# Zero borders written a layer earlier, a residual loaded in four pieces, and three fp32r products for each fp32 product in an attention layer's front

## The reference, cut to what matters

```python
# layer 0: attention with a bias net, then an MLP
x = x + out_proj(attention(...))
x = x + mlp_w2 @ gelu(mlp_w1 @ bn(x) + b1) + b2          # 512 -> 2048 -> 512
# layer 1: deformable 3x3 convolution under a gate
d   = normalise(pointwise(depthwise3x3(x[:, :256])))     # mean and variance over the pixels
off = conv3x3(d, off_w)                                  # 18 channels: an offset (y, x) per tap
dc  = sum over 9 taps of dc_w[tap] @ bilinear(d at (y, x) + tap + off)
das = d * sigmoid(layernorm_channels(dc))
x   = x * das + x * g                                    # g: a gate from x[:, 256:]
# layer 2: linear attention
x   = x + gamma * ((Kf V) Qf / norm)
# layer 3: group norm, q, k, v, softmax attention, projection
h   = group_norm(x); q, k, v = W_qkv @ h + b
x   = x + W_out @ softmax(q k / 8) v
```

## Time and profile before

| | |
|---|---|
| median of 3 runs | 4279.25 us (4275.34 to 4280.5) |
| the profiled execution's own time | 4278.21 us |
| its span (first to last instruction) | 4276.4 us |
| PE, DVE, ACT, POOL busy | 91, 69, 60, 49% of the span |
| MLP stage ends, layer 1 begins | about 2721 us into the span |
| layer 1 ends, layer 2 begins | about 3438 us |
| front of layer 3, V and QK products | 3585 to 3751 us |

### The profile page before, as it was taken

One profiled execution on the slowest core, in us unless ns is written; L12 is line 12 of the kernel. 1 busy time (PEld: TensorE's weight loads), 2 busy tenths in 40 slices (PEclk: granted clock), 3 DMA queues, 4 the chain that ended last, 5 costly groups with the idle time before them and its releaser, 6 DMA issues. The chain is left out here.

```text
span 4276.4 us, 66562 instructions
## 1 busy us (share of the span) xinstructions
PE 3904.4 (91%) x18504; PEld 2388.6 (56%) x18504; DVE 2967.6 (69%) x4476; ACT 2575.5 (60%) x4592; POOL 2083.5 (49%) x1857
## 2 busy tenths in 40 slices
PE   5999999999999999999998999888779377969999
PEld 3555555555555555555556888547667243435553
DVE  7888888888888888888886333538898833235552
ACT  5899999999999999999994333322112420113331
POOL 0555555555555555555552555216676500036663
PEclk8999999999999999999999999989889677989999
DMA  1200000000000000000002000239999812453312
GB/s 48 101 12 10 9 9 11 10 10 9 9 12 9 10 9 9 12 10 9 9 9 82 1 1 1 79 101 377 367 370 393 299 47 71 145 128 70 70 41 79
DMA packets 146916, 326.80 MB, mean 76 GB/s; under 512 B 45736, under 2 KB 46760, under 8 KB 145788
## 3 DMA queue, kind: packets, MB, share of 16 engines
q1 hardware_dynamic: 105340, 174.46, 13.2%
q0 software_dynamic: 41472, 151.01, 9.0%
HBM read 246.14 MB, written 79.04 MB: 76 GB/s over the span
## 5 line engine op out<-in xcount | busy, mean ns | idle before, releaser
L557 POOL TENSOR_TENSOR cpb_sum<-cpb_tab 128x512 f32<-128x512 f32 x1028 | 1045.9, 1048 | 965.3 <-DVE cpb_r L687 965.0
L668 ACT ACTIVATE cpb_h<-cpb_z,net_vec 128x512 f32<-128x512 f32 x1536 | 1006.0, 697 | 50.5 <-PE cpb_z L608 37.9
L605 PE MATMUL cpb_z<-cpb_r,cpb_w2a 128*128 128x512 f32 x2048 | 858.5, 419 | 23.5 <-DVE cpb_h L728 23.5
L687 DVE SCALAR_TENSOR_TENSOR cpb_r<-cpb_sum,cpb_r 128x512 fp32r<-128x512 f32 x1024 | 695.5, 710 | 187.8 <-ACT cpb_r L662 187.8
L606 PE MATMUL cpb_z<-cpb_r,cpb_w2b 128*128 128x512 f32 x2048 | 801.1, 391 | 0.0
L608 PE MATMUL cpb_z<-cpb_r,cpb_w2a 128*128 128x512 f32 x2048 | 799.7, 390 | 0.0
L687 DVE SCALAR_TENSOR_TENSOR cpb_r<-cpb_z,cpb_r 128x512 fp32r<-128x512 f32 x1028 | 661.8, 685 | 160.4 <-ACT cpb_r L662 154.6
L662 ACT ACTIVATE cpb_r<-cpb_z 128x512 fp32r<-128x512 f32 x1028 | 560.5, 604 | 127.7 <-PE cpb_z L592 127.7
L662 ACT ACTIVATE cpb_r<-cpb_sum 128x512 fp32r<-128x512 f32 x1024 | 598.5, 648 | 2.0 <-POOL cpb_sum L557 2.0
L605 PEld LDWEIGHTS cpb_z<-cpb_r,cpb_w2a 128*128 128x128 f32 x2048 | 383.9, 187 | 365.8 <-issue 301.0
L1559 DVE SCALAR_TENSOR_TENSOR dc_acc<-dc_g,dc_wt,dc_acc 128x512 f32<-128x512 f32 x560 | 444.7, 800 | 58.0 <-DMA dc_g<-conv_out,dc_idx 42.0
(11 more groups left out here) (344 smaller groups left out, 5196.7 us busy)
## 6 DMA issues: line engine op xcount, KB each, us to landing
conv_out<-dc_ys SPq DMA_DIRECT2D x576, 64.0 KB, 6.1
cpb_log<-log_dram SPq DMA_DIRECT2D x66, 256.0 KB, 3.1
qk_parts<-gn_r SPq DMA_DIRECT2D x64, 256.0 KB, 2.0
dc_wr<-in_dc_wT SPq DMA_DIRECT2D x9, 1024.0 KB, 6.0
bias_dram<-cpb_bst SPq DMA_DIRECT2D x520, 8.0 KB
net_x<-in_x SPq DMA_DIRECT2D x8, 1024.0 KB, 9.4
sa_qa<-qk_parts SPq DMA_DIRECT2D x16, 512.0 KB
sa_ka<-qk_parts SPq DMA_DIRECT2D x16, 512.0 KB
```

The lines of the kernel that those rows point to most:

```text
L557: pool.tensor_tensor(SUM[:, r, :].rearrange("p (y x) -> p y x", x=W), TAB[:, slot, r, 0, :].unsqueeze(1).broadcast_to([P, NF // W, W]), TA ...
L605: pe.matmul(z2[:, bank, :], W2A[:], R1[:, k, :], start=True, stop=False)
L668: act.activation(H2[:, t % 8, :], z2[:, t % 3, :], ACT.Relu, bias=V("cpb_b2")).then_inc(h2a, 1)
L687: v.scalar_tensor_tensor(R2[:, t % RING, :], first_layer(t), 0.0, R1[:, t % RING, :].bitcast(F32), ALU.max, ALU.subtract).then_inc(r2_read ...
```

## The change

1. The border writes move from layer 1's SP list to the MLP stage's. There GpSimd clears a zero tile of half the width (128 x 256) first, SP writes 18 DMAs of the same bytes from it, and waits for them at the stage's end. In layer 1 weights(1) follows directly on the loads of OFW; GpSimd's and SP's waits for `borders` go.
2. In layer 1 GpSimd clears only the edge cells of DP that are read (two memsets of 544 and 512 values a partition) in place of the whole tile; ZERO's memset goes. ScalarE's wait for `zeroed` goes, TensorE waits for it before the offset convolution.
3. X comes back in four DMAs of 1 MB, a column block each: the first where the one of 4 MB was, the others when 129, 136 and 140 tiles have been sampled. VectorE waits for each piece before the first output of its block.
4. Layer 3's W_V and W_QK are split in high and low fp32r parts in layer 2: 12 casts of 128 x 512 on ScalarE after its work on image 0, 12 subtractions on GpSimd after column block 1. The low parts are written over the whole ones.
5. The front writes the normalised x as HH and HL (fp32r): ScalarE writes FULL (fp32, 128 x 512, a ring of four), VectorE casts it to HH and subtracts for HL, in 16 `parts`; six of them ahead of the V chunks, one after each of the first ten. V and QK are three fp32r products where there was one of fp32.

```diff
 def layer0_mlp
+        ZERO = s.sb("zero", [P, C // 2])
         @block.sync
+            sp.wait_ge(blank, 1)
+            for rows in itertools.chain(*g["conv_out"]):
+                for r0 in (0, HP * HP - edge):
+                    sp.dma_start(rows[r0:r0 + edge, :]..., ZERO[0:edge, :]...).then_inc(borders, 16)
+                sp.dma_start(middle..., ZERO[0:gaps, :]...).then_inc(borders, 16)
             for sem in g["spent"]:
                 sp.sem_clear(sem)
+            sp.wait_ge(borders, 16 * 18)
         @block.gpsimd
+            pool.memset(ZERO[:], 0.0).then_inc(blank, 1)
 def layer1
         @block.sync
-            for u in range(SLOTS):
-                for b in range(B):
-                    rows = table[u][b]
-                    sp.dma_start(rows[0:edge, :], ZERO[0:edge, :]).then_inc(borders, 16)
-                    sp.dma_start(rows[HP * HP - edge:, :], ZERO[0:edge, :]).then_inc(borders, 16)
-                    sp.dma_start(middle, ...).then_inc(borders, 16)
             weights(1)
...
             sp.wait_ge(y_mm, TILES)
-            sp.dma_start(X[:].rearrange("p t n -> p (t n)"), x_spill).then_inc(x_back, 16)
-            sp.wait_ge(borders, 16 * 3 * SLOTS * B)
+            for n, units in enumerate((0, LAST[1] + 1, LAST[2] - 4, LAST[3] - 4)):
+                cols = slice(n * NF, (n + 1) * NF)
+                if units:
+                    sp.wait_ge(sampled, units)
+                sp.dma_start(X[:, :, cols], x_spill.rearrange(...)[:, :, cols]).then_inc(x_back[n], 16)
         @block.gpsimd
-            pool.memset(DP[:], 0.0).then_inc(zeroed, 1)
+            pool.memset(images[:, :, 1:H + 3:H + 1, 1:W + 3], 0.0).then_inc(zeroed, 1)
+            pool.memset(images[:, :, 2:H + 2, 1:W + 3:W + 1], 0.0).then_inc(zeroed, 1)
             pool.memset(OFW[:], 0.0).then_inc(zeroed, 1)
-            pool.memset(ZERO[:], 0.0).then_inc(zeroed, 1)
...
-            pool.wait_ge(borders, 16 * 3 * SLOTS * B)
         @block.tensor
+            pe.wait_ge(zeroed, 3)
         @block.scalar
-            act.wait_ge(zeroed, 1)
         @block.vector
-                if n == 0 and m == 0:
-                    v.wait_ge(x_back, 16)
+                if m == 0:
+                    v.wait_ge(x_back[n], 16)
 def layer2
         @block.gpsimd
+                if n == 1:
+                    for i, (whole, high, low) in enumerate(PIECES):
+                        pool.wait_ge(split_h, i + 1)
+                        pool.tensor_tensor(low, whole, high.bitcast(F32), ALU.subtract).then_inc(split_l, 1)
         @block.scalar
+                if b == 0:
+                    act.wait_ge(weights_in, 64)
+                    for whole, high, low in PIECES:
+                        act.copy(high, whole).then_inc(split_h, 1)
 def layer3_front
         @block.tensor
+            def three(out, w, wl, x, xl, first, last):
+                pe.matmul(out, w, x, start=first, stop=False)
+                pe.matmul(out, wl, x, start=False, stop=False)
+                return pe.matmul(out, w, xl, start=False, stop=last)
             for i in range(CHUNKS):
-                pe.wait_ge(hn_a, CT // 2 * (i // NC + 1))
-                pe.wait_ge(hn_v, CT // 2 * (i // NC + 1))
...
                 for k in range(CT):
-                    mm = pe.matmul(pv[:, i % 2, :], HN[:, k, i * P:(i + 1) * P], WV[:, k, :], ...)
+                    if i % CT == 0:
+                        pe.wait_ge(hh_ready, i + k + 1)
+                        pe.wait_ge(hl_ready, i + k + 1)
+                    mm = three(pv[:, i % 2, :], HH[:, k, pix], HL[:, k, pix], WVH[:, k, :], WVL[:, k, :], ...)
...
-                        mm = pe.matmul(pq[:, m % RING, :], WQK[:, k, m * P:(m + 1) * P], HN[:, k, bass.ds(n * NF, NF)], ...)
+                        mm = three(pq[:, m % RING, :], WQH[:, k, of], WQL[:, k, of], HH[:, k, col], HL[:, k, col], ...)
         @block.scalar
+            for i in range(NT * CT):
+                n, m = divmod(i, CT)
+                if i >= CT:
+                    act.wait_ge(hl_ready, i - CT + 1)
+                act.activation(FULL[:, m, :], X[:, m, n * NF:(n + 1) * NF], ACT.Identity, ...).then_inc(full, 1)
         @block.vector
+            def parts(i):
+                n, m = divmod(i, CT)
+                v.wait_ge(full, i + 1)
+                v.tensor_copy(HH[:, m, col], FULL[:, m, :]).then_inc(hh_ready, 1)
+                v.wait_ge(hh_ready, i + 1)
+                v.tensor_tensor(HL[:, m, col], FULL[:, m, :], HH[:, m, col].bitcast(F32), ALU.subtract).then_inc(hl_ready, 1)
+            AHEAD = CT + 2
+            for i in range(AHEAD):
+                parts(i)
             v.sem_inc(r2_ready, RING)
             for i in range(CHUNKS):
...
                 v.tensor_tensor(VE[:, i % RING, :], pv[:, i % 2, :], BV[:], ALU.add).then_inc(v_ready, 1)
+                if i + AHEAD < NT * CT:
+                    parts(i + AHEAD)
```

More of the change, by code:

```diff
@@ L1 @@
 from contextlib import ExitStack
+import itertools
 import math
@@ L883, in layer0_mlp @@
         FULL = s.sb("full", [P, 2, NF])
+        ZERO = s.sb("zero", [P, C // 2])
+        blank, borders = s.sem("blank"), s.sem("borders")
         py = s.ps("py", [P, CT, NF])
@@ L911, in _ @@
         def _(sp):
+            sp.wait_ge(blank, 1)
+            HP = H + 4
+            edge, gaps = 2 * HP + 2, H - 1
+            for rows in itertools.chain(*g["conv_out"]):
+                for r0 in (0, HP * HP - edge):
+                    sp.dma_start(rows[r0:r0 + edge, :].rearrange("r (k c) -> r k c", k=2),
+                                 ZERO[0:edge, :].unsqueeze(1).broadcast_to([edge, 2, C // 2])).then_inc(borders, 16)
+                middle = rows[edge + W:edge + W + gaps * HP, :].rearrange("(y x) c -> y x c", x=HP)[:, 0:4, :]
+                sp.dma_start(middle.rearrange("y x (k c) -> y (x k) c", k=2),
+                             ZERO[0:gaps, :].unsqueeze(1).broadcast_to([gaps, 8, C // 2])).then_inc(borders, 16)
             for sem in g["spent"]:
                 sp.sem_clear(sem)
+            sp.wait_ge(borders, 16 * 18)
         @block.tensor
@@ L1125, in layer1 @@
         GA = s.sb("ga", [P, CT, B, 2])
-        ZERO, DCB = s.sb("zero", [P, C]), s.sb("dcb", [P, C])
+        DCB = s.sb("dcb", [P, C])
         LM, LR, LN = (s.sb("lm", [P, NT, 4, 2]), s.sb("lr", [P, NT, 4]), s.sb("ln", [P, NT, 4]))
@@ L1132, in layer1 @@
         x_spill = nc.dram_tensor("x_spill", (P, CT * TOK), F32).ap()
-        table = [[nc.dram_tensor(f"conv_out{u}{b}", (HP * HP, C), F32).ap() for b in range(B)] for u in range(SLOTS)]
+        table = g["conv_out"]
         ORDER = [(tap, b) for tap in range(TAPS - 2) for b in range(B)] + [(tap, b) for b in range(B)
@@ L1161, in layer1 @@
         n_mm, sig, d_whole, gated, x_back, x_ready = (s.sem("n_mm"), s.sem("sig"), s.sem("d_whole"), s.sem("gated"),
-                                                      s.sem("x_back"), s.sem("x_ready"))
+                                                      [s.sem(f"x_back{n}") for n in range(NT)], s.sem("x_ready"))
         block = s.block()
@@ L1649, in layer2 @@
         norms = [pq[:], pk[0:D].rearrange("p c d -> p (c d)")]
+        split_h, split_l = s.sem("split_h"), s.sem("split_l")
         block = s.block()
+        PIECES = ([(g["W_V"][:, k, :], g["W_PARTS"][2][:, k, :], g["W_PARTS"][3][:, k, :]) for k in range(CT)] +
+                  [(g["W_QK"][:, k, c:c + NF], g["W_PARTS"][0][:, k, c:c + NF], g["W_PARTS"][1][:, k, c:c + NF])
+                   for k in range(CT) for c in (0, NF)])
         @block.sync
@@ L1844, in layer3_front @@
         NC, HEADS, RING = HW // P, C // DH, 4
-        HN = s.sb("hn", [P, CT, TOK])
-        WQK, WV, BV, AVG = g["W_QK"], g["W_V"], g["B_V"], g["GROUP_AVG"]
+        BV, AVG = g["B_V"], g["GROUP_AVG"]
+        HH, HL = s.sb("hh", [P, CT, TOK], F32R), s.sb("hl", [P, CT, TOK], F32R)
+        WQH, WQL, WVH, WVL = g["W_PARTS"]
+        FULL = s.sb("full", [P, CT, NF])
         ST = s.sb("st", [P, CT, NT, 6])
@@ L1916, in _ @@
             act.wait_ge(step, 8)
-            for b in range(B):
-                for m in range(2, CT):
-                    act.activation(HN[:, m, b * HW:(b + 1) * HW], X[:, m, b * HW:(b + 1) * HW], ACT.Identity,
-                                   bias=SH[:, m, b:b + 1], scale=RS[:, m, b:b + 1]).then_inc(hn_a, 1)
+            for i in range(NT * CT):
+                n, m = divmod(i, CT)
+                if i >= CT:
+                    act.wait_ge(hl_ready, i - CT + 1)
+                act.activation(FULL[:, m, :], X[:, m, n * NF:(n + 1) * NF], ACT.Identity,
+                               bias=SH[:, m, n // 2:n // 2 + 1], scale=RS[:, m, n // 2:n // 2 + 1]).then_inc(full, 1)
             with act.Fori(0, NT) as n:
@@ L2470, in build @@
             g["prefetch"], g["prefetch_done"] = prefetch, lambda sp: sp.wait_ge(pre, 16 * (CT + 2))
+            g["conv_out"] = [[nc.dram_tensor(f"conv_out{u}{b}", ((H + 4) * (H + 4), C), F32).ap() for b in range(B)]
```

(1 more changed line is left out.)

37 lines of the change are left out of this document (20 added, 17 removed).

## The result

The changed kernel takes 4211.09 us (median of 4, 4208.98 to 4213.99); the kernel before took 4279.66 on the same chip (median of 4, 4275.34 to 4280.5). The ratio is 0.9842 (95% interval 0.9825 to 0.9859), 68.6 us less. The profiled execution took 4208.98, its span, from the first to the last instruction, is 4207.2, so 69.2 less than the span of before. The prediction was 4211, with 68.3 saved.

What follows compares the result with a forecast made beforehand. TensorE bounds the MLP stage and last layer's front, DMA the second layer's sampling. Savings of 25.9 + 7.8 - 0.3 + 34.9 = 68.3 us from 4278.2 give 4209.9, with the median's 1.04 4211; own range 4205 to 4216.

Steps and rivals of the forecast that it cites:

- Tap: Start of second layer: VectorE's first depthwise instruction no longer held by GpSimd's memset of DP, 7.0 us saved (bounds 5.6, 7.6).
- Clock gift: Second layer's pointwise products: with TensorE's idle cut, upper clock level throughout, 2.9 us saved (bounds 0 and 2.9).
- Stall: Second layer, first unit's chunks: weights(1) issued early ends TensorE's wait, 16.0 us saved before the first gather (bounds 13.2, 17.8).
- the 9.9: Start of second layer: total us by which the first main product (L1315) was to come earlier.
- Cover of the border writes: MLP stage: the 18 writes, 3.3 MB on SP, cost nothing, since nobody waits for them until the stage's end.
- X back: Second layer's sampling: x returned in four pieces leaves 1.6 us of VectorE's stall, 7.8 saved (bounds 0 and 9.4).
- Splits: Layer 2: splitting the last layer's weights on ScalarE and GpSimd costs 0.3 us by holding VectorE (bounds 0 and 3.1).
- Front: Last layer's front: three fp32r products replace two fp32 passes; V saves 11.9 us, QK 23.0, sum 34.9.
- B: Second layer's sampling: returning x in four gives nothing, as the same 4 MB run beside gathers; 4219 us, chance 0.12.
- D: Second layer: earlier gathering is not kept because something else paces sampling, 16 us lost; 4227 us, chance 0.05.
- E: Last layer's front: fp32r products run at the lower clock, front 79 us slower; 4325 us, chance 0.02.
- C: Second layer's start and layer 2: tap release and clock saving partly absent, splits hold VectorE 3 us; 4218 us, chance 0.12.

Runs made afterwards that it cites:

- two-product run: The changed kernel with two instead of three fp32r products in the last layer's front, low-part products left out: 4166.67 us (one execution).

## Why the prediction was right, point by point

The mechanisms held, as the points show. That the sum came out within 0.3 us (68.3 against 68.6) is luck on top (by the spans it is 69.2): by the table the parts missed by -1.2, +1.3, +0.2, +2.3 and +0.2 us, and two stages expected at nothing lost 1.9.

- **Tap.** 7.0 predicted, 6.2 measured. The term was mis-sized at the holding left: 0.6 assumed, 1.35 measured. The case taken as the bound (held through OFW's memset too, 5.6) is what happened: the tap ended 0.54 us after that memset. The rule of the Trainium skill (SBUF — State Buffer, Who interferes with whom) that the prediction set beside the row, waiting for the memset that has started, covers the memset of DP under way at 2723.79; that the tap did not get in between it and OFW's goes beyond the rule. The second memset of DP took 1.07 us, twice its estimate at the old rate, which the text had allowed for.
- **Clock gift.** 2.9 predicted, 2.7 measured (30.36 to 27.70); undoing the edges brought it back.
- **Stall.** 16.0 predicted, 17.3 to 17.5 measured, within its bounds; the whole slow stretch of the first four chunks went too, not only the stall. Together with the 1.2 missing ahead of it, the first gather is 26.0 earlier against 25.9. What the prediction had not said: the 9.9 and the 16.0 are not independent. The runs show two parallel chains, and without the borders' move what is won ahead of the first main product is worth nothing at the gather (148.6 us behind the tap against 148.3).
- **Cover of the border writes.** Right. In the MLP stage SP takes 91 us over their issue, beside products at a granted clock of 0.98 (0.96 there before), and nothing waits.
- **X back.** 7.8 predicted, 8.0 in the layer; 1.6 us of stall left predicted, 1.9 measured.
- **Splits.** Casts took 6.4 us (7.4 predicted), the subtractions 1.34 us each (1.56). Two holds on VectorE, as supposed, both hidden: 0 in place of 0.3. The measured +2.0 of layer 2 was in no step; it lies within the spread of that layer between runs of the same code (126.9 to 132.9).
- **Front.** V 11.3 (11.9 predicted, with an earlier start in it), Q and K 22.9 (23.0); the pitch is 0.2267 as taken from the MLP stage. The two-product run gives the same pitch and shows that no other engine is near.
- **Rivals.** B fell by the run with x in one piece, D by the run with the borders back, E by the clock of 1.00 in Q and K. Of C the tap's part is real at 0.8 us; the lower clock's and the splits' parts are not.

## What to carry to other kernels

Before adding up gains, ask which chains end at the same wait: here 10 us won on one chain were worth nothing until the other, a queue of cheap writes, had been cleared. A DMA in an in-order queue waits for the issue of what stands ahead of it; move the unhurried ones to a queue or a stage that nobody waits for. And before a matrix engine is made to do less, look at the rows where its granted clock is 0.50: here, products that nobody reads, put in the waits, and one load put first were worth 18 us on top of this change.

## What was not expected of the hardware

- The same 18 zero writes took 86 us to issue on SP in layer 1, 91 us there in the MLP stage, and 16 us on GpSimd's queue. Why an issue on SP takes so long (up to 12.81 us for one) no run shows. The mean DMA share was 0.10 in both stretches on SP, and it does not tell whether all 16 engines were nearly idle or one or two of them full.
- Three small memsets of 0.5 to 1.1 us in a row held one VectorE tap through all of them (2.62 us, with 2.16 for two), while the tap behind the 8.75 us memset did get in ahead of OFW's (it ended 0.55 us behind the first). OFW's memset then took 1.60 us in place of the 1.13 it takes where the tap is still waiting: it seems to have been held in its turn.
- The clock fell near 3482 though TensorE had paused at most 0.8 us, its last products being of 64 rows; with products of 128 x 128 in nearly the same places it stayed up, or fell later. Why it fell in one image's outputs and not in the other's is open.
- Layer 2's length varied by 6 us between runs of the same code, 5.3 of it in rows that a stretch at the lower clock lengthens. That is as much as a part of the change was worth.
